# Gate and up products of the sorted expert blocks: from one fp32 product to three fp32r products of split pairs

## What is computed

```python
scores = jnp.full_like(logits, -jnp.inf)
scores = scores.at[jnp.arange(T)[:, None], top_idx].set(top_vals)
scores = jax.nn.sigmoid(scores.astype(jnp.float32)).astype(logits.dtype)
xr = x[None, :, :] * scores.T[:, :, None]
gate_up = jnp.einsum('eth,ehf->etf', xr, gate_up_proj)
gate, up = jnp.split(gate_up, 2, axis=-1)
routed = jnp.einsum('etf,efh->eth', up * jax.nn.silu(gate), down_proj)
routed_sum = routed.sum(axis=0)
shared = jax.nn.silu(x @ shared_gate_w) * (x @ shared_up_w) @ shared_down_w
return (shared + routed_sum).reshape(orig_shape)
```

## Time and profile before

| what | value |
|---|---|
| median of the runs | 2739.33 us (2738.68 to 2741.82) |
| the profiled execution's own time | 2752.23 us |
| its span, first to last instruction | 2750.2 us |
| mean granted TensorE clock | 0.978 of full speed |
| TensorE matmuls busy | 2630.2 us, 96% |
| VectorE busy | 2046.9 us, 74% |
| ScalarE busy | 1621.7 us, 59% |
| GpSimd busy | 2140.3 us, 78% |

### The profile page before, as it was taken

The page is one execution under the profiler, slowest core; times in us unless marked ns, Lnnn a source line. Parts: engine busy times, 40 slices in busy tenths (PEclk is TensorE's granted clock), DMA queues, the critical chain, the costliest instruction groups (busy, mean ns, idle before and its releaser), DMA issues. The chain is left out here.

```text
span 2750.2 us, 32506 instructions
## 1 busy us (share of the span) xinstructions
PE 2630.2 (96%) x11020; PEld 1874.6 (68%) x11021; DVE 2046.9 (74%) x2916; ACT 1621.7 (59%) x1891; POOL 2140.3 (78%) x1106
## 2 busy tenths in 40 slices
PE   7986999899999999999999999999999999997898
PEld 2333677667777777777777777777777777765665
DVE  6766556578888888888888888888888888886111
ACT  2223323367767776776777677767767767774122
POOL 2543588479988998998899899889989988997233
PEclk9997899999999999999999999999999999999999
DMA  2001456200000000000000000000000000005421
GB/s 68 0 0 53 108 169 167 72 12 5 9 4 20 8 5 16 5 8 5 20 8 5 16 4 9 5 16 8 8 16 4 9 4 9 1 20 142 169 61 46
DMA packets 76126, 90.52 MB, mean 33 GB/s; under 512 B 9310, under 2 KB 64865, under 8 KB 75970
## 3 DMA queue, kind: packets, MB, share of 16 engines
q1 hardware_dynamic: 72994, 81.30, 10.3%
q0 software_dynamic: 2976, 7.22, 0.8%
HBM read 62.39 MB, written 27.02 MB: 33 GB/s over the span
## 5 line engine op out<-in xcount | busy, mean ns | idle before, releaser
L1925 DVE TENSOR_TENSOR at_top<-at_psum_s,at_top 128x512 f32<-128x512 f32 x960 | 662.7, 690 | 215.5 <-ACT at_prob L1832 194.0
L1832 ACT ACTIVATE at_prob<-at_psum_s 128x1024 f32<-128x1024 f32 x512 | 521.4, 1018 | 452.2 <-PE at_psum_s L932 449.0
L2053 POOL TENSOR_TENSOR at_p_lo<-at_prob,at_p_hi 128x1024 fp32r<-128x1024 f32 x256 | 616.3, 2408 | 2.0 <-ACT at_p_hi L1846 2.0
L1914 DVE TENSOR_TENSOR at_prob<-at_prob,at_psum_m 128x1024 f32<-128x1024 f32 x512 | 603.5, 1210 | 0.0
L1838 ACT ACTIVATE at_prob<-at_prob 128x1024 f32<-128x1024 f32 x512 | 537.7, 1050 | 9.9 <-DVE at_prob L1914 6.7
L2082 POOL TENSOR_TENSOR at_acc<-at_acc,at_prob 128x1024 f32<-128x1024 f32 x189 | 453.1, 2397 | 82.8 <-ACT at_prob L1838 73.0
L1747 PE MATMUL at_psum_o<-at_prob,at_v 128*128 128x512 f32 x1024 | 483.4, 594 | 1.8 <-DVE at_oT_lo L1946 1.4
L2086 POOL TENSOR_TENSOR at_acc<-at_acc,at_prob 128x1024 f32<-128x1024 f32 x189 | 454.3, 2404 | 0.0
L930 PE MATMUL at_psum_s<-at_q_hi,sw_gate_up_hi 128*128 128x512 f32 x1024 | 403.4, 394 | 5.1 <-DVE sw_gate_up_lo L1906 5.1
L932 PE MATMUL at_psum_s<-at_q_hi,sw_gate_up_lo 128*128 128x512 f32 x1024 | 401.6, 392 | 0.0
L931 PE MATMUL at_psum_s<-at_q_lo,sw_gate_up_hi 128*128 128x512 f32 x1024 | 401.4, 392 | 0.0
(11 more groups left out here) (350 smaller groups left out, 4486.9 us busy)
## 6 DMA issues: line engine op xcount, KB each, us to landing
ef_gate_up<-in_ef_gate_up SPq DMA_DIRECT2D x8, 1024.0 KB
at_wq_split<-lf_pieces SPq DMA_DIRECT2D x8, 512.0 KB, 2.9
at_wk_split<-lf_pieces SPq DMA_DIRECT2D x8, 512.0 KB, 4.8
at_wv_split<-lf_pieces SPq DMA_DIRECT2D x8, 512.0 KB, 2.9
at_wo_split<-lf_pieces SPq DMA_DIRECT2D x8, 512.0 KB, 4.5
ef_down<-in_ef_down SPq DMA_DIRECT2D x8, 512.0 KB
ef_rows_in<-ef_zeros SPq DMA_DIRECT2D x23, 128.5 KB, 9.0
ef_rows<-ef_rows_in SPq DMA_DIRECT2D x23, 128.5 KB, 2.2
```

Of the source, the lines that this page charges most:

```text
L1832: nc.scalar.activation(pair(u, c, half), psum_s[:, 2 * half:2 * half + 2, :], ACT.Copy).then_inc(kept, 1)
L1914: nc.vector.tensor_tensor(part, part, psum_m[:].unsqueeze(1).to_broadcast([P, 2, BT]), ALU.subtract).then_inc(shifted, 1)
L1925: nc.vector.tensor_tensor(top[:, u % 2, :], psum_s[:, t, :], top[:, u % 2, :], ALU.max).then_inc(maxed, 1)
L2053: nc.gpsimd.tensor_tensor(p_lo[:, at, :], part, p_hi[:, at, :].bitcast(F32), ALU.subtract).then_inc(p_lo_ready, 1)
```

## The change

For blocks 1 to 22 the gate and up products are done as three fp32r products of split pairs. Block 0 stays as it was (`first_product`, with its own buffer `first_rows`).

- The rows are split: ScalarE writes `rows_hi` from `psum_xt` (`take_rows_hi`, in the place of `copy_rows`), and VectorE writes `rows_lo` = `psum_xt` - `rows_hi` (`take_rows_lo`, new).
- The weights are split for each block again: ScalarE writes `w_hi`, 128 x 2048 values of the block's expert (`split_hi`, new, two blocks ahead), and VectorE writes `w_lo` = `gate_up` - `w_hi` (`split_lo`, new). Both have two buffers, which are laid over `x_hi` and `x_lo`.
- ScalarE and VectorE each read the expert's number into a register of their own once per block (TENSOR_LOAD). TensorE still does so for `down`, and no longer for the gate and up halves from block 1 on.
- TensorE waits for `parts_hi` and `parts_lo` at the start of a block (two counts of each per block) in place of `rowsT_ready`.
- The loops are gone: all 22 steps are written out on TensorE and ScalarE.
- In the first block some semaphores are merged (`constants`, `chosen`), with the same waits.

The diff, without the merging of semaphores in the first block:

```diff
@@ -2132,10 +2133,10 @@
         rows_zeroed = semaphore("ef_rows_zeroed")
         tokens_stored = semaphore("ef_tokens_stored")
         scattered = moves.scattered
-        rows, rowsT = alloc("ef_rows", [P, 2, W]), alloc("ef_rowsT", [P, 2, NC, P])
+        rows, first_rows = alloc("ef_rows", [P, 2, W]), alloc("ef_first_rows", [P, NC, P])
         rows_loaded = [semaphore(f"ef_rows_loaded{k}") for k in range(2)]
         x_transposed = semaphore("ef_x_transposed")
-        rowsT_ready = semaphore("ef_rowsT_ready")
+        first_rows_ready = semaphore("ef_first_rows_ready")
 
         def load_rows(sp, j):
             sp.dma_start(rows[:, j % 2, :], rows_in[j * P:(j + 1) * P, :]).then_inc(rows_loaded[j % 2], 16)
...
@@ -2486,6 +2487,9 @@
             hidden = sb("ef_hidden_x", [P, 2, F])
             hiddenT = sb("ef_hiddenT", [P, 2, NF, P])
             result = sb("ef_result", [P, 2, D])
+            rows_hi, rows_lo = (sb(f"ef_rows_{part}", [P, 2, NC, P], F32R) for part in ("hi", "lo"))
+            w_hi, w_lo = (part[:].rearrange("p c t -> p (c t)").rearrange("p (k c n) -> p k c n", k=2, c=NC)
+                          for part in (x_hi, x_lo))
             psum_xt = ps("ef_psum_xt", [P, NC, P])
             psum_gu = ps("ef_psum_gu", [P, 2, 2, F])
             psum_ht = ps("ef_psum_ht", [P, NF, P])
@@ -2498,17 +2502,13 @@
             d_psum = semaphore("ef_d_psum")
             result_ready = semaphore("ef_result_ready")
             ids_ready = semaphore("ef_ids_ready")
+
+            parts_hi = semaphore("ef_parts_hi")
+            parts_lo = semaphore("ef_parts_lo")
             gathered, rows_stored = moves.gathered, moves.rows_stored
 
-            def steps(eng, body):
-
-                body(1, 1, True)
-                body(2, 0, True)
-                with eng.Fori(1, NBK // 2 - 1) as pair:
-                    body(pair * 2 + 1, 1, True)
-                    body(pair * 2 + 2, 0, True)
-                body(NBK - 2, 1, True)
-                body(NBK - 1, 0, False)
+            def expert(eng, j):
+                return eng.value_load(block_expert[0:1, j:j + 1], min_val=0, max_val=E - 1)
 
             with nc.Block() as block:
                 @block.sync
@@ -2522,25 +2522,31 @@
                 def _(pe):
                     pe.wait_ge(experts_loaded, 16 * 2 * E)
 
-                    def expert(j):
-                        return pe.value_load(block_expert[0:1, bass.ds(j, 1)], min_val=0, max_val=E - 1)
-
-                    def product(half, k, e):
+                    def first_product(half, e):
+
                         for c in range(NC):
                             wt = gate_up[:, bass.ds(e, 1), c, bass.ts(half, F)].rearrange("p a n -> p (a n)")
-                            last = nc.tensor.matmul(psum_gu[:, k, half, :], rowsT[:, k, c, :], wt,
+                            last = nc.tensor.matmul(psum_gu[:, 0, half, :], first_rows[:, c, :], wt,
                                                     start=(c == 0), stop=(c == NC - 1))
                         last.then_inc(gu_psum, 1)
 
-                    def transpose_hidden(j, k):
+                    def product(j, half):
+                        k, part = j % 2, bass.ts(half, F)
+                        for c in range(NC):
+                            last = three(nc, psum_gu[:, k, half, :], rows_hi[:, k, c, :], rows_lo[:, k, c, :],
+                                         w_hi[:, k, c, part], w_lo[:, k, c, part], start=(c == 0), stop=(c == NC - 1))
+                        last.then_inc(gu_psum, 1)
+
+                    def transpose_hidden(j):
                         pe.wait_ge(hidden_ready, j + 1)
                         for c in range(NF):
-                            last = nc.tensor.transpose(psum_ht[:, c, :], hidden[:, k, bass.ts(c, P)], ident[:])
+                            last = nc.tensor.transpose(psum_ht[:, c, :], hidden[:, j % 2, bass.ts(c, P)], ident[:])
                         last.then_inc(h_transposed, 1)
 
-                    def down_product(j, k, e):
+                    def down_product(j, e):
+                        k = j % 2
                         pe.wait_ge(hiddenT_ready, j + 1)
-                        if not isinstance(j, int) or j >= 2:
+                        if j >= 2:
                             pe.wait_ge(result_ready, j - 1)
                         for c in range(NF):
                             wt = down[:, bass.ds(e, 1), c, :].rearrange("p a n -> p (a n)")
@@ -2548,49 +2554,62 @@
                                                     start=(c == 0), stop=(c == NF - 1))
                         last.then_inc(d_psum, 1)
 
-                    def step(j, k, more):
-                        e = expert(j)
-                        pe.wait_ge(rowsT_ready, j + 1)
-                        product(0, k, e)
-                        transpose_hidden(j - 1, 1 - k)
-                        product(1, k, e)
-                        if more:
-                            transpose_rows(pe, psum_xt, 1 - k, (j + 1 - (1 - k)) * 8 + 16)
-                        down_product(j - 1, 1 - k, expert(j - 1))
-
-                    e = expert(0)
-                    pe.wait_ge(rowsT_ready, 1)
-                    product(0, 0, e)
-                    product(1, 0, e)
+                    e = expert(pe, 0)
+                    pe.wait_ge(first_rows_ready, 1)
+                    first_product(0, e)
+                    first_product(1, e)
                     transpose_rows(pe, psum_xt, 1, 16)
-                    steps(pe, step)
-                    transpose_hidden(NBK - 1, 0)
-                    down_product(NBK - 1, 0, expert(NBK - 1))
+                    for j in range(1, NBK):
+                        before_e = expert(pe, j - 1)
+                        pe.wait_ge(parts_hi, 2 * j)
+                        pe.wait_ge(parts_lo, 2 * j)
+                        product(j, 0)
+                        transpose_hidden(j - 1)
+                        product(j, 1)
+                        if j + 1 < NBK:
+                            transpose_rows(pe, psum_xt, (j + 1) % 2, (j + 1) // 2 * 16 + 16)
+                        down_product(j - 1, before_e)
+                    transpose_hidden(NBK - 1)
+                    down_product(NBK - 1, expert(pe, NBK - 1))
 
                 @block.scalar
                 def _(act):
-                    def copy_rows(j, k):
+                    act.wait_ge(experts_loaded, 16 * 2 * E)
+
+                    def take_rows_hi(j):
                         act.wait_ge(x_transposed, j + 1)
-                        nc.scalar.activation(rowsT[:, k], psum_xt[:], ACT.Copy).then_inc(rowsT_ready, 1)
-
-                    def silu(j, k):
+                        if j >= 3:
+                            act.wait_ge(gu_psum, 2 * (j - 2) + 2)
+                        nc.scalar.activation(rows_hi[:, j % 2], psum_xt[:], ACT.Copy).then_inc(parts_hi, 1)
+
+                    def split_hi(j):
+                        e = expert(act, j)
+                        if j >= 3:
+                            act.wait_ge(gu_psum, 2 * (j - 2) + 2)
+                        nc.scalar.activation(w_hi[:, j % 2].rearrange("p c n -> p (c n)"),
+                                             gate_up[:, bass.ds(e, 1)].rearrange("p a c n -> p (a c n)"),
+                                             ACT.Copy).then_inc(parts_hi, 1)
+
+                    def silu(j):
                         act.wait_ge(gu_psum, j * 2 + 1)
-                        nc.scalar.activation(silu_g[:, k, :], psum_gu[:, k, 0, :], ACT.Silu).then_inc(silu_ready, 1)
-
-                    def copy_hidden(j, k):
+                        nc.scalar.activation(silu_g[:, j % 2, :], psum_gu[:, j % 2, 0, :], ACT.Silu).then_inc(silu_ready, 1)
+
+                    def copy_hidden(j):
                         act.wait_ge(h_transposed, j + 1)
-                        nc.scalar.activation(hiddenT[:, k], psum_ht[:], ACT.Copy).then_inc(hiddenT_ready, 1)
-
-                    def step(j, k, more):
-                        silu(j, k)
-                        copy_hidden(j - 1, 1 - k)
-                        if more:
-                            copy_rows(j + 1, 1 - k)
-
-                    silu(0, 0)
-                    copy_rows(1, 1)
-                    steps(act, step)
-                    copy_hidden(NBK - 1, 0)
+                        nc.scalar.activation(hiddenT[:, j % 2], psum_ht[:], ACT.Copy).then_inc(hiddenT_ready, 1)
+
+                    split_hi(1)
+                    silu(0)
+                    take_rows_hi(1)
+                    split_hi(2)
+                    for j in range(1, NBK):
+                        silu(j)
+                        copy_hidden(j - 1)
+                        if j + 1 < NBK:
+                            take_rows_hi(j + 1)
+                        if j + 2 < NBK:
+                            split_hi(j + 2)
+                    copy_hidden(NBK - 1)
 
                 @block.vector
                 def _(dve):
```

(29 more changed lines are left out.)

14 lines of the change are left out of this document (6 added, 8 removed).

## The result

| what | before | changed |
|---|---|---|
| median of the runs | 2739.33 us (2736.57 to 2741.82, 5 runs) | 2725.43 us (2721.01 to 2726.04, 5 runs) |
| ratio to the kernel before | | 0.9945, 95% interval 0.9931 to 0.9960 |
| span of the profiled execution | 2750.2 us | 2724.3 us |

The account below looks back on a forecast made before the run. TensorE alone was taken to set the pace, at 5.82 us a block. Cheaper products (-14.1 us) and a later start (+0.6) gave -13.5 us, from 2739.3 to 2725.8 us, range 2721 to 2737.

Parts of the forecast that it names:

- The products: TensorE, 22 blocks: 12 fp32r products (2.80 us) replace 4 fp32 products (3.44 us), 0.64 us saved a block, 14.1 in all.
- The sum: Whole kernel: -14.1 us for products and +0.6 at the start, -13.5 us, from 2739.3 to 2725.8 us.
- A change between fp32 and fp32r costs nothing: TensorE, twice a block: switching between fp32 and fp32r products was costed at nothing.
- The splits fit beside TensorE: ScalarE and VectorE: row and weight splits end in time; narrowest room 0.22 us, for the block after the next.
- The start, +0.6 us: Block 1 must wait for rows_lo(1), which stands behind gate(0) on VectorE: 2611.80 in place of 2611.23.
- Rival 1: Splits set the pace but the kernel still gains: 2732.4 us by register load, 2734.8 by indirect DMA; chance 0.19.
- Rival 2: VectorE becomes the bound, split_lo taking 4.37 us and blocks 6.38: slower, 2752.2 us; chance 0.07.
- GpSimd's work costs nothing on the path: Indirect DMAs on GpSimd, two blocks ahead, at 1.03 us each, were costed at nothing.
- The pitch: TensorE's fp32r products of 512 columns: 0.233 us each taken from measured rows, against the skill's 215.7 ns.

Follow-up runs that it names:

- splits beside fp32 products: Changed kernel with all splits and waits kept, but gate and up as fp32 products from rows_hi and unsplit weights; ratio 1.0001 to the kernel before.
- the last experiment: Changed kernel with rows_lo of block 1 put ahead of the gate of block 0 on VectorE; ratio 0.9944 to the kernel before.
- the kernel with 4.5 us: Changed kernel with the whole split_lo subtraction done twice, first into a spare buffer; ratio 1.0022 to the kernel before.
- the halves' subtractions: Changed kernel with split_lo as two subtractions of 1024 columns each instead of one of 2048; ratio 0.9939 to the kernel before.

## Why the prediction was right, and where it was not

- *The products.* Right: 12 x 0.233 for 4 fp32 products, 0.64 us a block. Measured 43 halves at 0.322. Two kernels that differ in the form of the products (splits beside fp32 products, 126.10, and the changed one, 112.27) give 13.83 us, so this term is the whole gain.
- *The sum.* The traces give 44 x 0.322 = 14.2 us for the products and 0.5 at the start, 13.7 in all, against 13.5 forecast. That the two medians agree to 0.4 us is luck, as their interval is 11 to 19 us wide. The forecast also expected the profiled execution 12.9 us above the median in both kernels; in the changed one it was 0.6 above (2726.04 against 2725.43). The 2725.8 did not need this, as it was counted from the median.
- *A change between fp32 and fp32r costs nothing.* Right: a block is the plain sum of its parts, 5.175 us.
- *The splits fit beside TensorE.* Right, shown by taking them away (no gain) and by adding them alone (no loss). The room was given as 0.22 us for two blocks and was 0.5 to 0.6. Two steps were too long in it: the register load stands only 0.27 us behind the rows' copy, not 0.47, since part of it runs beside the copy; and `rows_lo` starts 0.61 us behind the start of `gate` (2645.08 - 2644.47), not 0.69.
- *The start, +0.6 us.* The size was nearly right, the gap grew by 0.5 us, from 0.56 to 1.06. The reason was only half right: I put all of `gate` ahead of `rows_lo` into the sum, and the last experiment shows that it runs beside the rows' copy. What block 0 itself takes (5.39 and 5.12 us here, 3.70 to 6.76 over all ten profiled executions) was not in the sum at all; it goes by the granted clock and not by the change, and it varies by more than this whole term.
- *Rival 1 (register load on ScalarE up to 1.28 us, or one indirect DMA ahead of `split_lo`).* Neither cost anything. The load is 0.28; once in 22 blocks `split_hi` came 0.3 us late, which the room took up. An indirect DMA did start ahead of `split_lo` twice, a gather 0.33 us ahead of the first one and the scatter 0.02 ahead at 2657.96, and it did not hold it up: `split_lo` took 2.291 to 2.303 us in all 22 blocks.
- *Rival 2 (VectorE the bound, slower).* The mechanism exists but did not set in: the price of 1.09 us for 512 columns did not come up beside GpSimd's indirect DMAs. Its point of decision was wrong, though. I had 3.80 us for `split_lo` by VectorE's circle with two hand-overs in it. The runs show that the chain of two blocks comes first, at (7.5 + S) / 2, for which 5.82 means a `split_lo` of about 4.1 us (3.9 with the late register load of the slower pairs); the kernel with 4.5 us was slower by 0.22%, not by the 0.5% of my sum.
- *GpSimd's work costs nothing on the path.* Right in the time, but the forecast had it at 1.03 an operation; for the scatters it is 2.9. The Trainium skill ("SBUF — State Buffer", section "Who interferes with whom") has the contention of two SBUF inputs with GpSimd, and the trace agrees in one direction, 2.91 against 1.03 us. Its rule that the earlier one holds the port to the end does not show for VectorE. Halves that started with a scatter pending took no longer, nor did the second of two subtractions (2.29 us from 2652.83) beside the scatter that had begun at 2651.48 in the kernel with `split_lo` twice. And `split_lo` took 2.30 us from 2657.98, with the scatter in its issue since 2657.96. One of the halves' subtractions, with the scatter 0.08 us ahead of it, began 0.50 us behind `split_hi` in place of 0.14; another, with the scatter 0.10 ahead, began on time. What delayed the one is open. The scatters at 2657.96 and in the other blocks fit a GpSimd that needs the port only at the start of its issue, which no experiment here took apart.
- *The pitch.* The Trainium skill's 215.7 ns for 512 columns ("TensorE: Matmul & The Clock Gate", section "Wait — 56ns, not 53.3ns?") did not appear here either; the products stand 0.23 us apart. Why was not looked for.

## What to carry to other kernels

When one engine is busy all the time, its own rows give the gain of cheaper work to a per cent or so; what has to be found out is whether everything hung on the other engines ends in time, and that is a sum along the longest circle of hand-overs, which can span two blocks. A busy share of 73% (VectorE, 75.9 of 103.5 us) still had only 0.5 to 0.6 us of room in 10.35. To price an addition that nearly fits, add a known amount of the same work and see how much of it comes out.

## What the runs showed of the hardware that I had not expected

- An indirect DMA's issue on GpSimd grows from 1.03 to 2.91 us when a VectorE subtraction with two SBUF inputs (2.29 us) has started ahead of it, to 1.85 when the subtraction is cut in two, and stays at 1.03 beside an equally long VectorE operation with one SBUF input. It ends 0.9 us behind the end of the subtraction that was running at its start. When it starts 0.02 us ahead of the subtraction it takes 1.03. VectorE's operations stay at their length in all these cases (2.28 to 2.31 us, and 1.22 for halves).
- The first register load of each engine in the stretch takes 1.09 to 1.14 us, all later ones of the two kernels 0.27 to 0.31.
- Behind 2.9 us without a matmul the same eight matmul records took 3.70 us at a granted clock of 1.00 in one execution and 5.39 at 0.68 in another.
- Two profiled executions differ by 12.0 us in stages that the change leaves alone, nearly as much as the change is worth; why was not looked for. The stretch that the change touches repeats to 0.01 us between kernels.
